# Map stage of a fused image block on one Trainium2 core: the second norm's broadcast and scaling move into the convolution, the fc2 products between the transposes

## Chip, core and metric

The kernel runs on one core of one Trainium2 chip. The metric is the time of one execution on the device in microseconds (us). The kernel before was timed three times; its time is the median of these runs.

## What is computed

The input is an image batch `x` (2, 96, 256, 256). A layer norm over channels is followed by windowed attention on overlapping 16x16 patches; then comes the part that this change touches, a per-pixel network with a depthwise convolution, and at last a small quantized network. Cut to the part that matters:

```python
y  = _layernorm(tok2, norm2_w, norm2_b)              # the "second norm", over 96 channels
y  = _gelu(y @ fc1_w + fc1_b)                        # fc1: 96 -> 192
dw = _gelu(depthwise_conv_5x5(y) + dw_b)             # 192 channels
tok2 = (y + dw) @ fc2_w + fc2_b + tok2               # fc2: 192 -> 96
x  = x + tok2                                        # outer residual
t  = x_tokens;  n = (t - mean(t)) / sqrt(var(t) + eps)   # the "third norm"
h  = relu(q_acc(q_mul(n) @ q_mul(W1).T) + q_mul(b1))     # 96 -> 384, fp8 products
x  = t + q_acc(q_acc(q_mul(h) @ q_mul(W2).T) + q_mul(b2))
```

## The kernel before

Three stages follow one another: `norm_stage`, `attention_stage` and `map_stage`. Only `map_stage` is touched. It works through the two images in 52 strips of 10 rows (26 for each image). The program of every engine is written out by hand: the order of the calls is the order of the work, and the engines meet through semaphores (`wait_ge`, `then_inc`). The loop runs over u = 0 to 50, the 52nd strip stands behind it.

One turn of the loop has a `first_half` and a `second_half`. It finishes strip u and, at places named `beside(...)`, prepares strip v = u + 1.

`first_half` on TensorE (`pe`):
- 12 products of fc1 for the pixels themselves (L1299), ScalarE puts them through Gelu into `Z` (L1391). Beside them run the variance sums of the second norm of strip v (`var2`, L1139).
- 6 groups (`NCG`) of 64 convolution matmuls as the profile counts them (L1312), in PSUM banks 0 and 1 or 2 and 3, with ScalarE's Gelu into `Z2` behind each (L1397). `gather2` (L1145) lies behind the first group. VectorE meanwhile turns the standard deviations into three bf16 parts of the reciprocal (`parts`, L1486 to L1493, the last one signals `dve_parts2`).
- 7 groups of transposes (L1328: six of 8, one of 4), alternating between banks 4, 5 and banks 6, 7. Behind each, VectorE adds the transposed convolution to `Z` (`back`, L1553, two instructions a group). A transpose group waits for the `back` of the group two before it.

`second_half` on TensorE:
- 6 products `fc2` (L1165, banks 0 and 1, `add_fc2` on VectorE at L1513 behind each) and between them 7 `spread2` (L1154, four bf16 matmuls each, banks 5 and 6), the broadcast of the reciprocals of the second norm of strip v. Behind each `spread2` VectorE scales two rows into `XN` (`scale2`, L1506). A `spread2` waits for the `scale2` two before it.
- The third norm: `mean3` (L1173), `centre3` on VectorE (L1518), squares on ScalarE (L1366), `var3` (L1179), `gather3` (L1185), the parts of the reciprocal on VectorE, `spread3` (L1191).
- The quantized network (`hidden` L1199, `output` L1207), and beside all of the third norm and this network the 26 `windows` (L1220) of strip v: fc1 on patches for the convolution, which ScalarE puts through Gelu into `Y1` (L1382).

SyncE stores the finished strip (L1048), once a strip. GpSimd adds the residuals (L1092, L1099) and copies the fc2 constant row (`means`, L1103). Before the loop the strip 0 is normed alone, with `spread2` and `scale2` following one another without other work.

The order of the calls in the second half before:

```python
fc2(nx, 0, n1)
fc2(nx, 1, n1)
beside(spread2, 0, 1)
fc2(nx, 2, n1)
beside(spread2, 2)
...
fc2(nx, 5, n1)
beside(spread2, 5, 6)
mean3(half3, n5, nx, 0)
mean3(half3, n5, nx, 1)
beside(windows, 0, 1)
```

Of the kernel before, what the change touches and what calls it, by code (L numbers as in the profile page):

```python
# [881 lines left out]
NF = TO // FT  # L882
XF = 43
NX = (W + XF - 1) // XF
NL = RI * W // FT
# [8 lines left out]
def map_stage(nc, x, n2w, n2b, fc1w, fc1b, dww, dwb, fc2w, fc2b, w1, b1, w2, b2, ident, pick, rep, spread, taps, inside,  # L894
# [3 lines left out]
    with ctx:  # L898
# [218 lines left out]
        def _(pe):  # L1117
# [106 lines left out]
            def second_half(n1, n5, nx, half3, v):  # L1224

                def beside(piece, *js):
                    if v is not None:
                        for j in js:
                            piece(v, j)

                fc2(nx, 0, n1)
                fc2(nx, 1, n1)
                beside(spread2, 0, 1)
                fc2(nx, 2, n1)
                beside(spread2, 2)
                fc2(nx, 3, n1)
                beside(spread2, 3)
                fc2(nx, 4, n1)
                beside(spread2, 4)
                fc2(nx, 5, n1)  # L1240
                beside(spread2, 5, 6)
                mean3(half3, n5, nx, 0)
                mean3(half3, n5, nx, 1)
                beside(windows, 0, 1)
                mean3(half3, n5, nx, 2)
                var3(n5, 0)
                beside(windows, 2)
                mean3(half3, n5, nx, 3)
                var3(n5, 1)
                beside(windows, 3)  # L1250
                mean3(half3, n5, nx, 4)
                var3(n5, 2)
                beside(windows, 4)
                var3(n5, 3)
                var3(n5, 4)
                beside(windows, 5)
                gather3(n1)
                beside(windows, 6)
                pe.wait_ge(dve_parts3, n1)
                spread3(n5, 0)  # L1260
                beside(windows, 7, 8)
                spread3(n5, 1)
                hidden(n5, 0)
                beside(windows, 9, 10, 11)
                spread3(n5, 2)
# [20 lines left out]
            def first_half(n13, n12, n6, n14, v):  # L1286

                def beside(piece, *js):
                    if v is not None:
# [14 lines left out]
                for q in range(NCG):  # L1304
# [32 lines left out]
            windows(0, *range(2 * NG))  # L1337
            with pe.Fori(0, nstrip - 1) as u:
                v = pe.snap(u + 1)
                first_half(pe.snap(u * (2 * NG)), pe.snap(u * (2 * NZ)), pe.snap(u * NCG), pe.snap(u * 14), v)  # L1340
                second_half(v, pe.snap(u * NF), pe.snap(u * NX), half_of(pe, u), v)
            last = nstrip - 1
            first_half(last * 2 * NG, last * 2 * NZ, last * NCG, last * 14, None)
            second_half(last + 1, last * NF, last * NX, half_of(pe, last), None)

        @block.scalar
        def _(act):
# [54 lines left out]
            def second_half(n1, n5, v):  # L1402
                def beside(*rs):
                    if v is not None:
                        windows(v, *rs)

                square3(n5, 0)
                square3(n5, 1)
                for j in range(2, NF):
                    beside(j - 2)  # L1410
                    square3(n5, j)
                beside(3)
                act.wait_ge(pe_rep3, n1)
                A.activation(STD3[:, :], P[0:C, 4, CV:2 * CV], ACT.Sqrt, bias=EPS[:, 0:1]).then_inc(act_std3, 1)

                beside(4, 5, 6, 7, 8)
                hidden16(n5, 0)
                beside(9, 10, 11)
                hidden16(n5, 1)
# [30 lines left out]
        def _(dve):  # L1450
# [104 lines left out]
            def first_half(n7, steps2, v):  # L1555
                if v is None:
                    back(n7, *range(NB))
                    return
                sum2(v)
                dve.wait_ge(act_std, v + 1)  # L1560
                parts(STD, RB[0], CV, steps2, dve_parts2)
                back(n7, *range(NB))

            def second_half(n1, n5, nx, half3, steps3, v):
                def beside(piece, *js):
                    if v is not None:
                        for j in js:
                            piece(v, j)

                dve.wait_ge(pool_x, n1)  # L1570
                add_fc2(half3, nx, 0)
                add_fc2(half3, nx, 1)
                beside(scale2, 0, 1)
                add_fc2(half3, nx, 2)
                beside(scale2, 2)
                add_fc2(half3, nx, 3)
                beside(scale2, 3)
                add_fc2(half3, nx, 4)
                beside(scale2, 4)
                add_fc2(half3, nx, 5)  # L1580
                beside(scale2, 5, 6)
                for j in range(NF):
                    centre3(half3, n5, j)
                sum3(n1, n5)
# [15 lines left out]
            with dve.Fori(0, nstrip - 1) as u:  # L1600
                v = dve.snap(u + 1)
                steps2 = dve.snap(u * (2 * VSTEPS) + (1 + VSTEPS))
                first_half(dve.snap(u * NB), steps2, v)
                second_half(v, dve.snap(u * NF), dve.snap(u * NX), half_of(dve, u), dve.snap(steps2 + VSTEPS), v)
            last = nstrip - 1
            steps3 = last * 2 * VSTEPS + 1 + VSTEPS
            first_half(last * NB, None, None)
            second_half(last + 1, last * NF, last * NX, half_of(dve, last), steps3, None)

# [65 lines left out]
```

## Time and profile before

| What | Value |
|---|---|
| Median of 3 runs | 8434.09 us (8430.1 to 8454.12) |
| Profiled execution, its time | 8441.3 us |
| Its span, first to last instruction | 8439.5 us |
| Mean granted TensorE clock | 0.975 of full speed |
| TensorE busy | 7670.8 us, 91% of the span |
| VectorE, ScalarE, GpSimd busy | 4919.9, 4683.4, 2161.9 us |

The span is cut into 40 slices on the profile's page. The attention stage ends in slice 19; the map stage fills the rest. All times in the rows below are counted in us from the span's start, and the line numbers are those of the kernel before. PE is TensorE, PEld its weight loads, DVE VectorE, ACT ScalarE, POOL GpSimd, SP SyncE.

### The profile page before, as it was taken

What the parts mean: (1) busy time and instruction counts of PE and PEld (TensorE: products, weight loads), DVE (VectorE), ACT (ScalarE), POOL (GpSimd) and SP (SyncE); (2) the same over time, 40 slices, a digit from 0 to 9 for tenths busy, and PEclk for the clock granted to TensorE, in tenths of its full rate; (3) what the DMA queues carried; (4) which work ended last, traced back from release to release, by engine and by line L of the source; (5) the groups of instructions that cost most, each with busy time, mean ns of one, the idle gap of its engine ahead of it and who ended that gap; (6) DMA issues with size and microseconds to landing.
All of it is one profiled execution on the core that took longest, in us unless ns stands there. A gap on an engine that the chain in (4) does not pass through costs nothing.

```text
span 8439.5 us, 205332 instructions
## 1 busy us (share of the span) xinstructions
PE 7670.8 (91%) x77004; PEld 4600.6 (55%) x77004; DVE 4919.9 (58%) x8231; ACT 4683.4 (55%) x7546; POOL 2161.9 (26%) x1712
## 2 busy tenths in 40 slices
PE   8969999999999999996989898989989898989898
PEld 3335555555455555554666666666666666666665
DVE  7867777777777777775344444444444444444444
ACT  6636555566565565653555454545454545455554
POOL 0023434434343343342112121212121212111111
PEclk9979999999999999997999999999999999999999
DMA  7734444444344443432111111111111111111110
GB/s 213 231 99 103 95 100 98 98 98 99 92 106 96 99 102 92 105 93 72 33 43 37 43 37 43 37 43 37 43 37 40 39 36 44 33 43 35 43 37 26
DMA packets 403125, 611.55 MB, mean 72 GB/s; under 512 B 95641, under 2 KB 338171, under 8 KB 377695
## 3 DMA queue, kind: packets, MB, share of 16 engines
q1 hardware_dynamic: 402639, 604.98, 28.9%
q8 instruction: 316, 5.18, 0.3%
q14 instruction: 170, 1.39, 0.1%
HBM read 395.33 MB, written 166.64 MB: 67 GB/s over the span
## 4 chain that ended last, share of the span: by engine, by line
PE 30%; DVE 10%; ACT 8%; issue 5%; DVEq 0%; SPq 0%; DMA 0%; ACTq 0%; POOLq 0%; POOL 0%
PE P L1299 6%; PE P L1165 6%; PE P L1312 5%; ACT H L1372 4%; PE P L1220 4%; DVE H L1538 3%; PE P L1173 3%; DVE H L1531 2%; PE P L1328 2%; DVE Z L1553 2%; PE P L1139 2%; ACT Z L1397 1%; ACT L1397 1%; ACT L1360 1%; PE P L1199 1%
## 5 line engine op out<-in xcount | busy, mean ns | idle before, releaser
L820 DVE TENSOR_REDUCE NM<-P 128x4 f32<-128x1024 f32 x1444 | 1764.8, 1222 | 596.3 <-PE P L654 591.7
L768 ACT ACTIVATE PROB<-P 128x1024 f32<-128x1024 f32 x1444 | 1400.2, 1021 | 1025.0 <-PE P L669 1025.0
L1220 PE MATMUL P<-FC,XN 97*126 97x192 f32 x5408 | 1099.0, 342 | 15.7 <-ACT Y L1382 14.8
L1220 PEld LDWEIGHTS P<-FC,XN 97*126 97x126 f32 x5408 | 941.3, 196 | 168.2 <-issue 77.8
L669 PE MATMUL P<-QF,KS 32*128 32x256 f32 x11552 | 834.5, 403 | 111.0 <-DVE QF L815 110.4
L1366 ACT ACTIVATE SQ<-Z 96x512 f32<-96x512 f32 x260 | 163.8, 630 | 1286.3 <-DVE Z L1518 1286.3
L669 PEld LDWEIGHTS P<-QF,KS 32*128 32x128 f32 x11552 | 525.4, 185 | 635.7 <-DVE QF L815 572.7
L505 POOL TENSOR_TENSOR Y<-XHS,RNS 96x512 f32<-96x512 f32 x304 | 600.6, 2003 | 811.8 <-DMA RNS<-rnorm 513.9
L677 PE MATMUL P<-PROB,V 128*32 128x256 f32 x11552 | 776.9, 386 | 1.4 <-ACT PROB L768 1.4
L1382 ACT ACTIVATE Y<-P 126x384 f32<-126x384 f32 x1352 | 704.1, 569 | 109.3 <-PE P L1220 104.2
L1099 POOL TENSOR_TENSOR T<-T,Y 96x512 f16 (+1 forms) x260 | 299.5, 1152 | 1720.0 <-DVE Y L1542 1720.0
L1103 POOL COPY Z<-T 1x2560 f32 (+1 forms) x52 | 236.9, 4555 | 1892.6 <-PE P L1165 1892.6
L1312 PE MATMUL P<-Y,WC 127*64 127x52 f32 x19968 | 625.2, 223 | 28.3 <-ACT Z L1397 28.3
L1312 PEld LDWEIGHTS P<-Y,WC 127*64 127x64 f32 x19968 | 598.9, 138 | 63.1 <-ACT Z L1397 34.9
L1553 DVE TENSOR_TENSOR Z<-P,Z 96x400 f32<-96x400 f32 (+1 forms) x728 | 342.6, 533 | 432.5 <-PE P L1328 432.5
L654 PE MATMUL P<-KB,QB 32*128 32x256 bf16 x5776 | 563.9, 272 | 20.1 <-DVE KB L810 16.9
L1299 PE MATMUL P<-XN,FC 97*96 97x440 f32 x1248 | 540.2, 554 | 0.7 <-ACT Y L1382 0.7
L645 PEld LDWEIGHTS P<-WQKV,Y 97*128 97x128 f32 x2888 | 377.5, 190 | 298.2 <-issue 298.2
L1165 PE MATMUL P<-Z,FC 97*96 97x430 f32 (+1 forms) x1248 | 499.4, 529 | 41.8 <-DVE Z L1553 41.8
L645 PE MATMUL P<-WQKV,Y 97*128 97x128 f32 x2888 | 515.4, 301 | 0.0
L1372 ACT ACTIVATE H<-P 128x1536 f16<-128x1536 f32 x260 | 377.4, 1451 | 238.7 <-DVE H L1538 182.8
L552 POOL TENSOR_TENSOR EDGE<-OS,RBC 128x160 f32<-128x160 f32 (+2 forms) x152 | 74.9, 493 | 1677.1 <-DMA RBC<-sums 1661.0
(152 smaller groups left out, 11706.8 us busy)
## 6 DMA issues: line engine op xcount, KB each, us to landing
RBC<-sums SPq DMA_DIRECT2D x456, 160.0 KB, 3.1
X<-x2map SPq DMA_DIRECT2D x52, 1344.0 KB, 8.3
XHS<-xhat SPq DMA_DIRECT2D x76, 768.0 KB, 6.2
RNS<-rnorm SPq DMA_DIRECT2D x38, 1536.0 KB, 9.4
x2map<-XHS SPq DMA_DIRECT2D x76, 768.0 KB
T<-in_x SPq DMA_DIRECT2D x52, 960.0 KB
out<-T SPq DMA_DIRECT2D x52, 960.0 KB, 4.9
X<-in_x SPq DMA_DIRECT2D x32, 1536.0 KB, 8.9
```

What stands on the lines that cost most here:

```text
L505: G.tensor_tensor(Y[0:C, x, :], XH[0:C, s % 2, :, x].rearrange("c r w -> c w r"), RN[:, :, x].rearrange("c r w -> c w r"), ALU.mult).then_ ...
L645: v = T.matmul(P[:, B_OV, PT + half * 128:PT + half * 128 + 128], yf[:, win(j, half * 128, half * 128 + 128)], WQKV[:, 128:256], start=Tru ...
L669: m = T.matmul(P[:, B_ST[h], half * PT:(half + 1) * PT], KS[hr, win(j, half * 128, half * 128 + 128)], QF[hr, :], start=True, stop=True)
L677: m = T.matmul(P[32 * h:32 * h + 32, B_OV, 0:PT], V[:, par, half, 32 * h:32 * h + 32], PROB[:, par, h, half * PT:(half + 1) * PT], start=( ...
L768: A.activation(PROB[:, par, u:u + 2, :], P[:, B_ST[u]:B_ST[u] + 2, :], ACT.Exp, scale=DQ ** -0.5).then_inc(act_exp, 1)
L820: V_.tensor_reduce(NM[:, :, :].rearrange("p a (u d) -> p u a d", d=32)[:, 2 * i:2 * i + 2, :, DQ], P[:, B_S[0]:B_S[0] + 2, :].rearrange("p ...
L1165: m = M.matmul(P[0:C, j % 2, 0:px.stop - px.start], FC2[0:C + 1 - half, half, :], Z[0:C + 1 - half, half, px], start=(half == 0), stop=(ha ...
L1220: m = M.matmul(P[0:KW, 5 + (r + 2) % 3, i * MLP:(i + 1) * MLP], xnf[:, RI * WX * w:RI * WX * w + KW], FC1[:, :], start=True, stop=True)
L1299: M.matmul(P[0:C, 6 + k % 2, 0:(x1 - x0) * RO], FC1[:, half * C:(half + 1) * C], XN[:, 2 + x0:2 + x1, 2:2 + RO], start=True, stop=True).th ...
L1312: m = M.matmul(P[64 * half:64 * half + 64, 2 * (q % 2) + i // GP, (i % GP) * NWIN:(i % GP + 1) * NWIN], WC[:, (half * C + c) * MW:(half * ...
L1372: A.activation(H16[:, :, :], P[:, 0:3, :], ACT.Copy).then_inc(act_h, 1)
L1382: A.activation(Y1[0:KW, :, 2 * r:2 * r + 2], P[0:KW, 5 + (r + 2) % 3, 0:2 * MLP].rearrange("p (w c) -> p c w", w=2), ACT.Gelu).then_inc(ac ...
```

## The change

On TensorE the 7 `spread2` leave the stretch of `fc2` and stand behind the last three groups of the convolution (0 and 1, then 2 and 3, then 4, 5 and 6). The transposes now wait for all 7 `scale2` of strip v, since they reuse banks 5 and 6. From the third group of transposes on, one `fc2` follows each group: it waits for the `back` of the group before. The two `windows` 0 and 1 stand ahead of the first `mean3`, and each later one up to 6 moves one place forward, so that `windows` 6 is issued ahead of `gather3`. VectorE does the 7 `scale2` ahead of `back`, and each `add_fc2` behind a `back`. ScalarE takes `windows` 0 ahead of the first square.

```diff
@@ second_half, TensorE
-                fc2(nx, 0, n1)
-                fc2(nx, 1, n1)
-                beside(spread2, 0, 1)
...
-                fc2(nx, 5, n1)
-                beside(spread2, 5, 6)
+                beside(windows, 0, 1)
                 mean3(half3, n5, nx, 0)
                 mean3(half3, n5, nx, 1)
-                beside(windows, 0, 1)
+                beside(windows, 2)
                 mean3(half3, n5, nx, 2)
...
-                beside(windows, 5)
+                beside(windows, 6)
                 gather3(n1)
-                beside(windows, 6)
                 pe.wait_ge(dve_parts3, n1)
@@ first_half, TensorE
+                    if q >= NCG - 3:
+                        beside(spread2, *((0, 1), (2, 3), (4, 5, 6))[q - NCG + 3])
+
+                if v is not None:
+                    pe.wait_ge(dve_xn, v * NL + NL)
                 pe.wait_ge(act_conv, n6 + NCG)
-                if v is not None:
-                    hold(pe, pe_passed, act_std, v + 1)
                 for q in range(NB):
...
                     m.then_inc(pe_zt, 1)
+                    if q >= 2:
+                        pe.wait_ge(dve_z, n14 + 2 * q)
+                        fc2(nx, q - 2, n1)
                 pe.wait_ge(dve_z, n14 + 14)
+                fc2(nx, NX - 1, n1)
@@ second_half, ScalarE
+                beside(0)
                 square3(n5, 0)
                 square3(n5, 1)
                 for j in range(2, NF):
-                    beside(j - 2)
+                    beside(j - 1)
                     square3(n5, j)
-                beside(3)
+                beside(4)
@@ first_half, VectorE
+                if v is not None:
+                    sum2(v)
+                    dve.wait_ge(act_std, v + 1)
+                    parts(STD, RB[0], CV, steps2, dve_parts2)
+                    for j in range(NL):
+                        scale2(v, j)
                 dve.wait_ge(pool_x, n1)
+                for q in range(NB):
+                    back(n7, q)
+                    if q >= 3:
+                        add_fc2(half3, nx, q - 3)
+                for j in range(NB - 3, NX):
+                    add_fc2(half3, nx, j)
```

No matmul, vector or activation instruction is added or taken away; only their places change.

TensorE at the end of the convolution, in the loop (L1301 is the convolution in the changed file, L1154 is `spread2`, L1319 are the transposes, which were L1328):

```order
+L1154 MATMUL P<-RB,BSEL 96x128 x8
+L1295 REGISTER_ALU
+L1301 MATMUL P<-Y,WC 64x52 x32
+L1154 MATMUL P<-RB,BSEL 96x128 x8
+L1295 REGISTER_ALU
+L1301 MATMUL P<-Y,WC 64x52 x32
+L1154 MATMUL P<-RB,BSEL 96x128 x12
+L1313 REGISTER_ALU
+L1319 MATMUL P<-IDN,Z 96x128 x16
```

The last three groups of the convolution now each have a block of `spread2` behind them, the last block with three of them right ahead of the transposes.

TensorE from the third transpose group on (L1165 is `fc2`):

```order
-L1165 MATMUL P<-Z,FC 96x430 x4
-L1154 MATMUL P<-RB,BSEL 96x128 x8
+L1319 MATMUL P<-IDN,Z 96x128 x8
+L1322 REGISTER_ALU
 L1165 MATMUL P<-Z,FC 96x430 x2
-L1154 MATMUL P<-RB,BSEL 96x128 x4
+L1319 MATMUL P<-IDN,Z 96x128 x8
+L1322 REGISTER_ALU
 L1165 MATMUL P<-Z,FC 96x430 x2
```

Where a `spread2` stood between two `fc2`, a transpose group and a wait now stand.

TensorE at the first `mean3` (L1173; L1220 are the `windows`):

```order
 L1165 MATMUL P<-Z,FC 96x410 x2
-L1154 MATMUL P<-RB,BSEL 96x128 x8
+L1214 ISA
+L1220 MATMUL P<-FC,XN 126x192 x4
 L1173 ISA
 L1173 MATMUL P<-T,MEANW 96x512
 L1173 ISA
 L1173 MATMUL P<-T,MEANW 96x512
-L1214 ISA
-L1220 MATMUL P<-FC,XN 126x192 x4
+L1220 MATMUL P<-FC,XN 126x192 x2
```

Two window pairs now stand between the last `fc2` and the first mean, in place of the last two `spread2`.

## Rows read from the trace of the kernel before

**Rows 1.** The page: span, and busy time of the engines.
```profile
span 8439.5 us, 205332 instructions
...
PE 7670.8 (91%) x77004; PEld 4600.6 (55%) x77004; DVE 4919.9 (58%) x8231; ACT 4683.4 (55%) x7546; POOL 2161.9 (26%) x1712
```

**Rows 2.** Timeline, SyncE's queue: stores of strips (start us, us, engine, line).
```profile
4193.53 0.36 SPq L1048 DMA_DIRECT2D out<-T  x1
...
5978.87 0.35 SPq L1048 DMA_DIRECT2D out<-T  x1
6064.06 0.36 SPq L1048 DMA_DIRECT2D out<-T  x1
6147.56 0.35 SPq L1048 DMA_DIRECT2D out<-T  x1
...
8273.59 0.36 SPq L1048 DMA_DIRECT2D out<-T  x1
```

**Rows 3.** Busy time by stretch: from:to, length, PE, PEld, DVE, ACT, POOL, PEclk.
```profile
6035.00:6037.70 2.70, 1.74 (x15) 1.70 (x16) 1.51 (x5) 1.53 (x4) 0.00 (x0) 1.00 0.00 0
6037.80:6041.20 3.40, 3.40 (x13) 2.75 (x12) 1.07 (x3) 2.42 (x3) 0.00 (x0) 0.50 0.00 0
...
6120.00:6124.00 4.00, 2.86 (x22) 2.55 (x23) 2.34 (x7) 2.46 (x6) 0.00 (x0) 1.00 0.00 0
```

**Rows 4.** Timeline, TensorE, end of the convolution and transposes (idle before, releaser).
```profile
6080.26 5.81 PE L1312 MATMUL P<-Y,WC 127*64 127x52 f32 x192 [0.56 <-ACT Z L1397]
6087.12 1.92 PE L1328 MATMUL P<-IDN,Z 128*96 128x128 f32 x16 [1.05 <-ACT Z L1397]
6089.40 2.01 PE L1328 MATMUL P<-IDN,Z 128*96 128x128 f32 x16 [0.36 <-DVE Z L1553]
```

**Rows 5.** The chain in order of time, fc2 and spread2 (start us, us, what).
```profile
6098.52 0.45 PE P L1154 x8
6098.97 1.48 PE P L1165 x4
6100.45 0.22 PE P L1154 x4
```

**Rows 6.** Timeline, TensorE, from the last two spread2 to spread3.
```profile
6105.31 0.61 PE L1154 MATMUL P<-RB,BSEL 96*96 96x128 bf16 x8
6106.54 1.95 PE L1173 MATMUL P<-T,MEANW 96*96 x4 [0.63 <-DVE T L1513]
6108.33 1.47 PE L1220 MATMUL P<-FC,XN 97*126 97x192 f32 x8
6109.63 1.02 PE L1173 MATMUL P<-T,MEANW 96*96 x2
6110.59 0.43 PE L1179 MATMUL P<-SQ,SSEL 96*32 96x128 f32 x8
...
6117.44 0.38 PE L1185 MATMUL P<-VS,REP 128*96 128x128 f32 x2
...
6121.14 0.42 PE L1191 MATMUL P<-RB,BSEL 96*96 96x128 bf16 x4 [2.67 <-DVE RB L1493]
```

**Rows 7.** Timeline, VectorE: last part of the second norm, first two `back` groups.
```profile
6080.49 0.22 DVE L1493 CAST RB<-RCP 32x128 bf16<-32x128 f32 x1
6088.21 2.01 DVE L1553 TENSOR_TENSOR Z<-P,Z 96x400 f32<-96x400 f32 x4 [7.50 <-PE P L1328]
```

**Rows 8.** Groups of instructions, VectorE, one strip (busy us, mean ns, idle before).
```profile
L1506 DVE TENSOR_TENSOR XN<-X,P 96x512 f32<-96x512 f32 x7 | 4.6, 683 | 0.0
L1513 DVE SCALAR_TENSOR_TENSOR T<-P,NW,T 96x430 f32 (+1 forms) x6 | 3.9, 658 | 4.0 <-PE P L1165 3.9
```

**Rows 9.** Timeline before the loop: last spread2, scale2 and first windows of strip 0.
```profile
3995.91 0.66 PE L1154 MATMUL P<-RB,BSEL 96*96 96x128 bf16 x4 [0.18 <-DVE XN L1506]
3996.61 0.69 DVE L1506 TENSOR_TENSOR XN<-X,P 96x512 f32<-96x512 f32 x1 [0.15 <-PE P L1154]
...
3997.45 0.97 PE L1220 MATMUL P<-FC,XN 97*126 97x192 f32 x2 [0.88 <-DVE XN L1506]
```

More of the change, by code:

```diff
@@ L1229, in beside @@
                             piece(v, j)
-                fc2(nx, 0, n1)
-                fc2(nx, 1, n1)
-                beside(spread2, 0, 1)
[L1234 to L1239, printed above, removed]
-                fc2(nx, 5, n1)
-                beside(spread2, 5, 6)
+                beside(windows, 0, 1)
                 mean3(half3, n5, nx, 0)
                 mean3(half3, n5, nx, 1)
-                beside(windows, 0, 1)
+                beside(windows, 2)
                 mean3(half3, n5, nx, 2)
                 var3(n5, 0)
-                beside(windows, 2)
+                beside(windows, 3)
                 mean3(half3, n5, nx, 3)
                 var3(n5, 1)
-                beside(windows, 3)
+                beside(windows, 4)
                 mean3(half3, n5, nx, 4)
                 var3(n5, 2)
-                beside(windows, 4)
+                beside(windows, 5)
                 var3(n5, 3)
                 var3(n5, 4)
-                beside(windows, 5)
+                beside(windows, 6)
                 gather3(n1)
-                beside(windows, 6)
                 pe.wait_ge(dve_parts3, n1)
@@ L1284, in second_half, with first_half @@
                 output(n5, 4)
-            def first_half(n13, n12, n6, n14, v):
+            def first_half(n13, n12, n6, n14, nx, n1, v):
                 def beside(piece, *js):
@@ L1339, in _ @@
                 v = pe.snap(u + 1)
-                first_half(pe.snap(u * (2 * NG)), pe.snap(u * (2 * NZ)), pe.snap(u * NCG), pe.snap(u * 14), v)
-                second_half(v, pe.snap(u * NF), pe.snap(u * NX), half_of(pe, u), v)
+                nx = pe.snap(u * NX)
+                first_half(pe.snap(u * (2 * NG)), pe.snap(u * (2 * NZ)), pe.snap(u * NCG), pe.snap(u * 14), nx, v, v)
+                second_half(v, pe.snap(u * NF), nx, half_of(pe, u), v)
             last = nstrip - 1
-            first_half(last * 2 * NG, last * 2 * NZ, last * NCG, last * 14, None)
+            first_half(last * 2 * NG, last * 2 * NZ, last * NCG, last * 14, last * NX, last + 1, None)
             second_half(last + 1, last * NF, last * NX, half_of(pe, last), None)
@@ L1409, in second_half @@
                 for j in range(2, NF):
-                    beside(j - 2)
+                    beside(j - 1)
                     square3(n5, j)
-                beside(3)
+                beside(4)
                 act.wait_ge(pe_rep3, n1)
                 A.activation(STD3[:, :], P[0:C, 4, CV:2 * CV], ACT.Sqrt, bias=EPS[:, 0:1]).then_inc(act_std3, 1)
-                beside(4, 5, 6, 7, 8)
+                beside(5, 6, 7, 8)
                 hidden16(n5, 0)
@@ L1553, in back, with first_half, second_half @@
                         V.tensor_tensor(z, p[:, 0:nw, half, 0:MW], z, ALU.add).then_inc(dve_z, 1)
[L1555 to L1568, printed above, removed]
-                dve.wait_ge(pool_x, n1)
[L1571 to L1581, printed above, removed]
+            def first_half(n7, steps2, half3, nx, n1, v):
+                if v is not None:
[4 more added lines that the diff above has]
+                        scale2(v, j)
+                dve.wait_ge(pool_x, n1)
+                for q in range(NB):
[4 more added lines that the diff above has]
+                    add_fc2(half3, nx, j)
+            def second_half(n1, n5, half3, steps3):
                 for j in range(NF):
@@ L1602, in _ @@
                 steps2 = dve.snap(u * (2 * VSTEPS) + (1 + VSTEPS))
-                first_half(dve.snap(u * NB), steps2, v)
-                second_half(v, dve.snap(u * NF), dve.snap(u * NX), half_of(dve, u), dve.snap(steps2 + VSTEPS), v)
+                half3 = half_of(dve, u)
+                first_half(dve.snap(u * NB), steps2, half3, dve.snap(u * NX), v, v)
+                second_half(v, dve.snap(u * NF), half3, dve.snap(steps2 + VSTEPS))
             last = nstrip - 1
             steps3 = last * 2 * VSTEPS + 1 + VSTEPS
-            first_half(last * NB, None, None)
-            second_half(last + 1, last * NF, last * NX, half_of(dve, last), steps3, None)
+            half3 = half_of(dve, last)
+            first_half(last * NB, None, half3, last * NX, last + 1, None)
+            second_half(last + 1, last * NF, half3, steps3)
 def constants():
```

## Prediction, made before the changed kernel was run

> **What bounds the kernel now.** I read the page first: TensorE is busy 91% of the span and no other engine over 58% [rows 1]. The store of each strip then gives the beat of the map stage: from 4193.53 to 8273.59 lie 48 strips, 85.00 us each on average [rows 2]. They are not equal: 85.19 us from 5978.87 to 6064.06, 83.50 us to the next [rows 2]. The view by stretches shows why. From 6037.8 to 6041.2 the granted clock is 0.50, which is the 1.2 GHz level, for 3.4 us in which TensorE works without a pause [rows 3]; in the shorter strip the same place, 6120 to 6124, stays at 1.00, the 2.4 GHz level [rows 3]. So one fall to 1.2 GHz costs 85.19 - 83.50 = 1.69 us, and the average strip holds (85.00 - 83.50) / 1.69 = 0.89 of one. The fall comes just behind the longest idle time that TensorE has in a strip, the 2.67 us in which it waits for the parts of the third norm [rows 6]. Everywhere in this part of the strip TensorE is busy or waits for VectorE, so its own timeline is the path: it is the sum that I make, from the fourth group of the convolution to the third mean.
>
> **The change, part by part.** I count from the start of the fourth convolution group, 6080.26 [rows 4]. Before, the transposes start at 6.86 (6087.12) [rows 4] and the third `mean3` at 29.37 (6109.63) [rows 6]. Now the new order.
>
> *Spreads in the convolution.* Three groups take 5.81 us less the 0.22 us tail of the last matmul, 1.87 us each [rows 4]. Two `spread2` take 0.45 us [rows 5]. A change between matmuls of 64 or 32 columns and of 96 seems to cost: a mean takes (6108.33 - 6106.54) / 2 = 0.90 us, but 0.96 us where the 32-column `var3` comes next [rows 6]; I take 0.09 for each change. The parts are ready at 0.45 (6080.71) [rows 7], far ahead of the first `spread2` at 1.96, and each `scale2` of 0.68 us [rows 8] finishes beside the next group. So the last group ends at 5.60 + 2 x 0.63 = 6.86. What follows has no cover: `spread2` 4 starts at 6.95, its four matmuls end 0.39 later, `scale2` 4 starts 0.04 behind them (3995.91 + 0.66 to 3996.61 [rows 9]) and ends at 8.06; `spread2` 6 waits for it, runs 0.42 as `spread3` does after a wait [rows 6], and `scale2` 6 ends at 9.25. A matmul starts 0.15 behind a `scale2` (3997.30 to 3997.45 [rows 9]). The transposes start at 9.40: 2.54 later than before.
>
> *fc2 between the transposes.* The first two groups and their `back` are unchanged, and the second `back` ends 6090.22 - 6087.12 = 3.10 behind the first transpose [rows 4, 7]. The third group fits in ahead of that, so the first `fc2` starts at 9.40 + 3.10 + 0.15 = 12.65. From there TensorE has work all the time: five `fc2` of about 1.45 (1.48 with the change to `spread2`) and one narrower of 1.39 (410 columns in place of 430), 8.6 us in all [rows 5], and four more transpose groups, 28 at 0.11 (16 start in 1.65 us [rows 4]), 3.1 us. VectorE needs 1.0 us for a `back` and 0.66 us for an `add_fc2` [rows 7, 8] against 2.3 us of TensorE a group; only the fifth `fc2` waits some 0.2 us for its bank. The last `fc2` is issued by 24.6.
>
> *Windows ahead of the mean.* Before, the first mean started 6106.54 - 6105.31 = 1.23 us behind the issue of the last `fc2`, 0.63 us of it a wait for `add_fc2` [rows 6]. Two windows take 1.30 us [rows 6] and fill just this: the first mean starts at 26.0. Two means take 1.79 us and one window 0.65 us: the third mean starts at 28.46, against 29.37. **That is 0.91 us less a strip.** One window more is then behind us, but it is the one that used to lie in the wait for the parts: from `gather3` to `spread3` pass 6121.14 - 6117.44 = 3.70 us before and after, as this is a chain over ScalarE and VectorE. TensorE's idle time in it grows from 2.67 to about 3.3 us, which costs nothing in itself. ScalarE's windows move by one with it and it has no more to do before the root. GpSimd's copy and SyncE's loads are released earlier, never later. Without any clock term the change is worth 51 x 0.91 = 46 us.
>
> *The clock.* The fall behind the third norm stays, its cause being longer. It now comes in every strip (0.89 before), while its start can also lie inside the idle time, which hides part of it: 0.8 to 1.69 us, about 1.5 on average, as before (0.89 x 1.69 = 1.50). New is idle time ahead of the transposes: TensorE stands still about 0.6 us before `spread2` 6 and 0.9 us before the transposes, with 0.4 us of work between. The kernel before has 1.05 us there and then 0.36 [rows 4] with no fall, and 2.67 us elsewhere with one. The new place lies between these rows, so its price runs from 0 to a fall in each strip. A fall there catches the two transpose groups that everything waits for: 16 transposes would take 3.3 to 3.5 us in place of 1.75, part of it is absorbed where group three waits for `back`, and 1.1 to 1.4 us are left, 1.2 in the mean. I take the fall: two idle times so close leave TensorE idle for most of 2 us, right behind a stretch of small matmuls, and before, too, nearly each strip had its fall from one single idle time. The Trainium skill, "TensorE: Matmul & The Clock Gate", section "A second HAM failure mode: psum-queue depth-cycling", says that short idle times between groups of matmuls, if frequent, are enough to make the clock swing between its levels. By that rule the sum is that with the second fall, without it the one under B; no row here shows a fall behind short idle times, so the trace neither agrees nor disagrees.
>
> **Sum.** A strip: 83.50 - 0.91 + 1.50 + 1.2 = 85.3 us, against 85.00. Over 51 strips +15 us; the last strip, which has no `spread2` to move and keeps the interleaving, gives back about 1. The profiled execution took 8441.3 us, 7 above the median of 8434.09, well inside the spread of the runs; I put the difference on the median: **8448 us, +0.17%**. A measurement of this kernel can tell about 0.3% (25 us) from no change, so this is "the same", 8409 to 8459.
>
> **Rivals.**
> - *A, the forecast:* the gain of 0.91 is there and a second fall in nearly each strip eats it. 8448 us, itself 8425 to 8462, since the fall's cost depends on where it starts. Chance 0.45.
> - *B, no second fall:* 1.5 us idle in two pieces are too little to drop the clock. For it: 1.05 + 0.36 us did not. Then 83.50 - 0.91 + 1.45 = 84.04 a strip, 8434 - 49 = 8385 us. If the fall comes in half the strips, about 8415. Chance together 0.33.
> - *C, slower:* each change between transposes and `fc2` costs what the change to 32 columns costs. There are 11 in a strip. At 0.09 us that is 1.0 us a strip, and with the second fall 8448 + 51 = 8499 us; it decides from 0.02 us a change (8459). Against it: between `spread2` and `fc2`, both 96 columns like the transposes, the chain shows no gap [rows 5]. New waits also stand at each change, for semaphores that came 0.1 to 1 us before. Chance 0.22. The Trainium skill, same page, section "Architectural detail: the array is 16× 32×32, not 1× 128×128", says that TensorE pulls weight loads ahead of running matmuls. By that rule the price of C is 0; the trace agrees for `fc2` and `spread2` (four matmuls in 0.22 us).
>
> That the change does not do what it says is no case here: the order of the calls is the order of the work, and the rows of the order show it.
>
> **How the numbers follow.** Faster 0.33 (B), same 0.45 (A), slower 0.22 (C). The range leaves out the upper part of C and the lower edge of B: 8378 to 8480. The likeliest case alone is 8425 to 8462.
>
> **What would show it.** In the profile after: the transposes start 9.4 us behind the fourth convolution group with idle times of about 0.6 and 0.9 us ahead of them; the third mean at 28.5 in a strip whose clock stays at 1.00 there; the idle time ahead of `spread3` is 3.3 us; a second stretch at 0.50 lies on the transposes in nearly each strip, and the 16 first transposes last about 3.4 us there. Strips come every 85.3 us. If no strip shows 0.50 on the transposes and the beat is 84.0, B is right; if clean strips show the third mean later than 29.0, C is, and the gaps between L1319 and L1165 will hold it. I am wrong altogether if VectorE, not TensorE, turns out late in the interleaved part, or if the fall behind the third norm disappears.

## The result, and the profile after

| | before | after |
|---|---|---|
| Median of 20 runs each | 8436.94 us (8430.1 to 8454.12) | 8451.48 us (8441.07 to 8465.49) |
| Ratio of the times, 95% interval | | 1.0016 [1.0009, 1.0022] |
| Profiled execution, its span | 8439.5 us | 8446.9 us |
| Mean granted TensorE clock | 0.975 | 0.964 |

One run of the changed kernel, 19892.7 us, was disturbed; it is left out of the range and the ratio, and the median without it is 8450.84 us. The change makes the kernel 14.5 us slower (13.9 without that run). This is clear of the noise, but less than the 0.3% (25 us) called "the same". The page of the changed kernel answers to [rows 1]: TensorE is busy 61 us longer with the same number of matmuls.

```profile
span 8446.9 us, 205540 instructions
...
PE 7731.9 (92%) x77004; PEld 4678.1 (55%) x77004; DVE 4925.3 (58%) x8231; ACT 4691.9 (56%) x7546; POOL 2161.1 (26%) x1712
```

SyncE's queue in the timeline, the stores of strips (start us, us, engine, line), against [rows 2]:

```profile
4186.54 0.36 SPq L1048 DMA_DIRECT2D out<-T  x1
...
5978.61 0.35 SPq L1048 DMA_DIRECT2D out<-T  x1
6063.94 0.36 SPq L1048 DMA_DIRECT2D out<-T  x1
...
7429.28 0.36 SPq L1048 DMA_DIRECT2D out<-T  x1
```

The strips now take the same time to within 0.1 us, but for the first. From 4186.54 to 7429.28 lie 38 of them, 85.33 us each; there is no shorter one any more, where before one in ten took 83.50. From the first transposes of the map stage to those of the strip before the last, 50 strips, pass 4252.0 us before (4044.6 to 8296.7) and 4268.4 us after (4040.1 to 8308.5): 16.4 us more. From there to the end it is 142.8 and 138.4, which is 4.4 less. Against that the transposes lie 2.8 us later in each strip by the new order, the first one too. 16.4 + 2.8 - 4.4 = 14.8 us, close to the difference of the medians. (In this pair of executions the stages ahead, which the change does not touch, ran 7.4 us shorter.)

TensorE's timeline of the changed kernel, end of the convolution and transposes (start us, us, ..., idle before and releaser), against [rows 4]:

```profile
6080.14 2.08 PE L1301 MATMUL P<-Y,WC 127*64 127x52 f32 x64 [0.56 <-ACT Z L1393]
6082.15 0.65 PE L1154 MATMUL P<-RB,BSEL 96*96 96x128 bf16 x8
6082.73 2.08 PE L1301 MATMUL P<-Y,WC 127*64 127x52 f32 x64
6084.73 0.65 PE L1154 MATMUL P<-RB,BSEL 96*96 96x128 bf16 x8
...
6088.52 0.42 PE L1154 MATMUL P<-RB,BSEL 96*96 96x128 bf16 x4 [0.56 <-DVE XN L1503]
6089.81 1.95 PE L1319 MATMUL P<-IDN,Z 128*96 128x128 f32 x16 [0.86 <-DVE XN L1503]
6092.12 1.05 PE L1319 MATMUL P<-IDN,Z 128*96 128x128 f32 x8 [0.36 <-DVE Z L1550]
6093.00 1.67 PE L1165 MATMUL P<-Z,FC 97*96 97x430 f32 x4
```

The transposes start 9.67 us behind the fourth convolution group (forecast 9.40), with 0.56 and 0.86 us of idle time ahead of them (forecast 0.6 and 0.9). The 16 first ones take 1.95 us, about as long as at 2.4 GHz in [rows 4] (1.92). From `fc2` on the rows have no idle time. The same view further on in the strip before, whose transposes start at 6004.47, against [rows 6]:

```profile
6023.24 1.02 PE L1173 MATMUL P<-T,MEANW 96*96 x2
...
6031.04 0.38 PE L1185 MATMUL P<-VS,REP 128*96 128x128 f32 x2
6034.75 0.66 PE L1191 MATMUL P<-RB,BSEL 96*96 96x128 bf16 x4 [3.33 <-DVE RB L1490]
```

The third mean starts 9.67 + 6023.24 - 6004.47 = 28.44 us behind the fourth convolution group; the forecast was 28.46. The idle time ahead of `spread3` is 3.33 (forecast 3.3). But `spread3` takes 0.66 us there, 0.42 in [rows 6]. The view by stretches says why (from:to, length, PE, PEld, DVE, ACT, POOL, clock, ...), against [rows 3]:

```profile
6002.00:6006.00 4.00, 2.58 (x28) 2.28 (x27) 2.32 (x4) 0.86 (x1) 0.00 (x0) 1.00 0.00 0
6031.50:6033.60 2.10, 0.00 (x0) 0.00 (x0) 1.49 (x4) 2.06 (x4) 0.00 (x0) 1.00 0.00 0
6033.70:6040.40 6.70, 5.65 (x22) 4.89 (x23) 2.28 (x6) 2.34 (x5) 0.00 (x0) 0.50 0.00 0
...
6119.10:6125.70 6.60, 5.62 (x22) 4.86 (x23) 2.21 (x6) 2.25 (x5) 0.00 (x0) 0.50 0.00 0
```

On the transposes (6002 to 6006) the clock is at its upper level, so the second fall of the forecast does not exist. The known fall behind the third norm has changed instead. It begins inside the idle time, 1.1 us ahead of `spread3`, and TensorE stays at 1.2 GHz for 6.8 us, where it was 3.4 us before. In the next strip it starts 85.33 us later, at the same place.

### The profile page after: what moved, and what is told of

It is laid out like the page before. It is cut to its first block, busy times and chain, and to the rows that moved or that the text cites. A ratio compares the mean times of both kernels' runs of the same rounds, so it can differ in the third digit from the quotient of the medians.

```text
span 8446.9 us, 205540 instructions
## 1 busy us (share of the span) xinstructions
PE 7731.9 (92%) x77004; PEld 4678.1 (55%) x77004; DVE 4925.3 (58%) x8231; ACT 4691.9 (56%) x7546; POOL 2161.1 (26%) x1712
## 4 chain that ended last, share of the span: by engine, by line
PE 33%; DVE 8%; ACT 7%; issue 4%; DVEq 0%; DMA 0%; SPq 0%; ACTq 0%; POOLq 0%; POOL 0%
PE P L1288 6%; PE P L1220 5%; PE P L1165 5%; PE P L1301 5%; ACT H L1368 4%; PE P L1319 3%; DVE H L1535 3%; PE P L1173 3%; DVE H L1528 2%; PE P L1139 2%; PE P L1154 1%; DVE XN L1503 1%; PE P L1191 1%; PE P L1199 1%; ACT L1393 1%
## 5 line engine op out<-in xcount | busy, mean ns | idle before, releaser
L1220 PE MATMUL P<-FC,XN 97*126 97x192 f32 x5408 | 1145.2, 352 | 15.8 <-ACT Y L1378 14.9
L1220 PEld LDWEIGHTS P<-FC,XN 97*126 97x126 f32 x5408 | 992.8, 205 | 188.0 <-issue 98.8
L1301 PE MATMUL P<-Y,WC 127*64 127x52 f32 x19968 | 646.5, 223 | 28.3 <-ACT Z L1393 28.3
L1301 PEld LDWEIGHTS P<-Y,WC 127*64 127x64 f32 x19968 | 607.1, 138 | 71.1 <-ACT Z L1393 34.9
L1165 PE MATMUL P<-Z,FC 97*96 97x430 f32 (+1 forms) x1248 | 497.2, 527 | 0.1
L1528 DVE TENSOR_SCALAR H<-H,BF 128x512 f16<-128x512 f16 x780 | 228.5, 349 | 406.2 <-ACT H L1368 406.2
```

The costliest lines, as they stand in the source:

```text
L1165: m = M.matmul(P[0:C, j % 2, 0:px.stop - px.start], FC2[0:C + 1 - half, half, :], Z[0:C + 1 - half, half, px], start=(half == 0), stop=(ha ...
L1220: m = M.matmul(P[0:KW, 5 + (r + 2) % 3, i * MLP:(i + 1) * MLP], xnf[:, RI * WX * w:RI * WX * w + KW], FC1[:, :], start=True, stop=True)
L1301: m = M.matmul(P[64 * half:64 * half + 64, 2 * (q % 2) + i // GP, (i % GP) * NWIN:(i % GP + 1) * NWIN], WC[:, (half * C + c) * MW:(half * ...
```

## The experiments

A stretch at 1.2 GHz is called a fall, and a strip or a kernel without one is called clean. Where a fall starts and how long it lasts comes from the granted clock in the view by stretches. All counts are of the 51 strips of the loop. The last strip, which runs behind the loop with nothing beside it, is left out; every kernel here has falls of 13 us and more in it. The runs are shown in three groups, each with the kernel before timed beside it (8437.05, 8439.9 and 8438.65 us).

### First group: what makes the fall longer?

Two theories on the doubled fall stood against each other. L: the idle time has grown from 2.67 to 3.33 us, and its length sets the fall's. T: the new idle times ahead of the transposes have a part in it.

**`windows` 6 back behind `gather3`**, which restores the idle time of 2.67 us (`windows` 2 to 5 move one place back too):

```diff
-                beside(windows, 2)
                 mean3(half3, n5, nx, 2)
                 var3(n5, 0)
-                beside(windows, 3)
+                beside(windows, 2)
...
-                beside(windows, 6)
+                beside(windows, 5)
                 gather3(n1)
+                beside(windows, 6)
```

> The changed kernel, but windows 6 stand behind gather3 again (windows 2 to 5 one place later), so that TensorE's idle time ahead of spread3 is 2.67 us in place of 3.33 us. The work of a strip is the same: a strip without a fall of the clock is expected at about 82.5 us. Theory L (the fall behind the third norm became twice as long, 6.8 us, because the idle time ahead of it grew): the fall is 3.4 us again and costs 1.5 to 1.7 us, strips of 84.1 us on average, 8385 us in all. Theory T (the idle time ahead of the transposes is enough for a fall of its own as soon as the first one is shorter): stretches at 0.50 on the transposes in most strips, strips near 85.3 us, 8445 us, no gain.

Measured: 8444.82 us, ratio 1.0007 [0.9997, 1.0018]. The timeline of SyncE (stores) has strips of two lengths in one execution:

```profile
4357.42 0.36 SPq L1048 DMA_DIRECT2D out<-T  x1
4439.57 0.35 SPq L1048 DMA_DIRECT2D out<-T  x1
4524.45 0.36 SPq L1048 DMA_DIRECT2D out<-T  x1
...
5974.19 0.35 SPq L1048 DMA_DIRECT2D out<-T  x1
6059.52 0.36 SPq L1048 DMA_DIRECT2D out<-T  x1
```

82.15 us is a clean strip, 84.88 the next, and later ones are all 85.33. Four stretches of this kernel:

```profile
4217.20:4220.50 3.30, 3.30 (x18) 3.08 (x16) 2.10 (x4) 0.00 (x0) 0.00 (x0) 0.50 0.85 213
4247.90:4251.30 3.40, 3.40 (x14) 2.73 (x13) 1.24 (x2) 1.14 (x2) 0.00 (x0) 0.50 0.00 0
4301.00:4304.50 3.50, 2.99 (x25) 2.71 (x26) 2.03 (x5) 0.00 (x0) 0.00 (x0) 1.00 0.58 131
6029.70:6036.40 6.70, 6.49 (x25) 5.71 (x26) 1.52 (x3) 2.56 (x4) 0.00 (x0) 0.50 0.00 0
```

And two places in TensorE's timeline:

```profile
4216.27 4.49 PE L1319 MATMUL P<-IDN,Z 128*96 128x128 f32 x24 [0.86 <-DVE XN L1503]
...
6029.91 0.66 PE L1191 MATMUL P<-RB,BSEL 96*96 96x128 bf16 x4 [2.67 <-DVE RB L1490]
```

The time is the one that T gave (8445), but its falls are not there. L is wrong: with 2.67 us of idle time the fall lasts 6.8 us too (6029.7 to 6036.4), once it starts ahead of `spread3`. T is right only in that there can be a fall on the transposes (4217.2 to 4220.5). A strip with it has a 3.4 us fall behind the third norm as well: 84.88 = 82.14 clean + 1.69 + 1.05, so a fall on the transposes costs 1.05 us, if the short one costs here what it costs before. Three of this kernel's strips have one, and in the changed kernel only the very first strip. The seven strips from the first long fall on last 84.87, 85.10, 85.22, 85.27, 85.30, 85.30 and 85.33 us, and the fall starts 28.65, 29.12, 29.35, 29.47, 29.53, 29.56 and 29.59 us behind the first transpose. As long as a strip is shorter than 85.33, the next fall comes that much later in its strip, less of it is hidden in the idle time, and the next strip is longer. At 85.33 this stands still.

**`windows` 7 moved from behind `spread3` 0 to behind `gather3`:**

```diff
                 gather3(n1)
+                beside(windows, 7)
                 pe.wait_ge(dve_parts3, n1)
                 spread3(n5, 0)
-                beside(windows, 7, 8)
+                beside(windows, 8)
```

> The changed kernel, with windows 7 issued between gather3 and spread3, so that the idle time is 2.67 us and 0.65 us of work more is out of the way: a strip without a fall at about 81.9 us. Theory L: falls of 3.4 us, 1.6 us each, strips of 83.5 us, 8355 us in all. Theory T: falls on the transposes in addition, in some half of the strips or more (1.2 us each) and strips of 84.5 us or so, 8405 us. If neither the idle time nor its length matters and the fall stays at 6.8 us: 84.7 us, 8415 us.

Measured: 8436.29 us, 1.0001 [0.9991, 1.0011], more than any of its three forecasts. With 2.67 us of idle time 43 falls behind the third norm last 6.8 us and 8 last 3.4. Their starts part them: all long ones start at most 0.35 us behind the start of `spread3`, all short ones at least 0.35 us behind it. The strips mostly take 85.25 us, but this kernel does not come to rest: the fall starts some 0.08 us later in each strip, until a short one comes (strips of 83.6 and 84.0 us) or one on the transposes beside the long one (86.2 us, four strips; the first strip has one too). The mean strip is 85.04, 0.29 less than in the changed kernel, and the moved window alone saves 0.26 by clean strips (second group). So this small saving shows, while the change's 0.95 does not. One of the falls on the transposes, by stretches (the transposes start at 4557.18):

```profile
4557.20:4560.50 3.30, 3.30 (x16) 3.15 (x17) 1.05 (x2) 0.00 (x0) 0.00 (x0) 0.50 0.54 135
```

**All `fc2` behind all transposes,** everything else as in the changed kernel:

```diff
-                    if q >= 2:
-                        pe.wait_ge(dve_z, n14 + 2 * q)
-                        fc2(nx, q - 2, n1)
                 pe.wait_ge(dve_z, n14 + 14)
-                fc2(nx, NX - 1, n1)
+                for j in range(NX):
+                    fc2(nx, j, n1)
```

> Only one part of the change undone: the six fc2 stand behind all transposes again, the rest as in the changed kernel. TensorE then has the three waits of about 0.3 us between transposes and 0.8 us ahead of the first fc2 again: a strip without a fall at 82.5 + 1.7 = 84.2 us. Theory L: idle 3.33 us ahead of spread3, fall of 6.8 us, 2.9 us: 87 us a strip, 8530 us. Theory T: the idle times ahead of and between the transposes now add up and there is a fall on them in most strips; 86.5 to 87 us, 8520 us, too, but with two stretches at 0.50 a strip. If the fall costs only 1.5 us: 85.7 us, 8470 us.

Measured: 8527.21 us, 1.0108 [1.0091, 1.0124]. Stores, then TensorE's `fc2` in the timeline:

```profile
6015.63 0.35 SPq L1048 DMA_DIRECT2D out<-T  x1
6101.76 0.36 SPq L1048 DMA_DIRECT2D out<-T  x1
6189.38 0.35 SPq L1048 DMA_DIRECT2D out<-T  x1
```
```profile
6135.92 8.86 PE L1165 MATMUL P<-Z,FC 97*96 97x430 f32 x24 [0.81 <-DVE Z L1548]
```

The waits for `back` that the interleaving covers are open again (0.81 us ahead of the first `fc2`, and two of 0.27 ahead of transposes). Strips with a short fall take 86.13 us, so a clean one would take 86.13 - 1.69 = 84.44, 1.9 more than in the changed order. Those with a long fall (22 of 51) take 87.6 to 87.8. The time is the one that L gave (8530), but by luck: L had a long fall in every strip. Rival C, by which switching between transposes and `fc2` costs more than it brings, has fallen. Here too the long falls start ahead of `spread3` or at most 0.31 us behind its start, the short ones from 0.35 us on.

**The windows' move alone, on the kernel before** (`windows` 0 and 1 ahead of the first mean, the later ones one place forward, ScalarE's the same):

```diff
                 beside(spread2, 5, 6)
+                beside(windows, 0, 1)
                 mean3(half3, n5, nx, 0)
                 mean3(half3, n5, nx, 1)
-                beside(windows, 0, 1)
+                beside(windows, 2)
```

> The kernel before with one part of the change alone: windows 0 and 1 ahead of the first mean, and windows 6 ahead of gather3. They cover the wait of 0.63 us ahead of the mean: a strip without a fall at 83.50 - 0.63 = 82.9 us. The idle time ahead of spread3 grows to 3.33 us here too, and nothing is changed ahead of the transposes (1.05 us idle). Theory L: the fall becomes 6.8 us long in most strips and costs 2.4 to 2.9 us, strips of 85.3 to 85.7 us, 8450 us or more: the part alone is no gain. Theory T (the length of that idle time is of no matter): fall as before, 1.5 us, strips of 84.4 us, 8405 us.

Measured: 8624.9 us, 1.0222 [1.0205, 1.0239]: far from what was expected. TensorE's timeline, and a stretch right behind:

```profile
6013.29 2.00 PE L1220 MATMUL P<-FC,XN 97*126 97x192 f32 x8 [1.69 <-DVE XN L1507]
6015.09 3.15 PE L1173 MATMUL P<-T,MEANW 96*96 x4
```
```profile
6014.30:6017.60 3.30, 3.30 (x7) 1.60 (x6) 0.56 (x1) 0.49 (x1) 1.57 (x1) 0.50 0.89 209
```

In the old order `scale2` 6 is the last thing in the stretch of `fc2`, and all windows wait for it. Ahead of the mean TensorE stands idle 1.69 us for it, and the whole third norm comes later; a second fall follows (in 50 strips), and the strips take 88.6 us, or 89.2 where the fall behind the third norm is a long one (12 of 51; those start 2.0 us or more ahead of `spread3`). The windows can only go ahead of the mean because the change has `scale2` finished in the convolution. The parts of this change can't be priced one at a time on the kernel before.

### Second group: the idle times filled

If the clock is what takes the gain, the gain must appear where it doesn't fall. Two f32 matmuls of 512 columns are put into the wait for the third norm's parts. Their output is not read by anyone.

```diff
+            def fill(bank, *ns):
+                for n in ns:
+                    M.matmul(P[0:C, bank, 0:n], MEANW[:, :], WC[0:C, 0:n], start=True, stop=True)
...
                 gather3(n1)
+                fill(0, 512, 512)
                 pe.wait_ge(dve_parts3, n1)
```

> The changed kernel with two idle-filling matmuls of 96x96x512 f32 behind gather3, 0.9 us each, whose output nobody reads. They shorten TensorE's idle time ahead of spread3 from 3.33 to about 1.6 us and end ahead of the parts, so no work is late. Theory I (the idle time in the third norm is what drops the clock): the fall there disappears; what is left are the falls ahead of the transposes that the first strips of the run with windows 6 behind gather3 showed (each with 1.1 us of cost, in up to half of the strips): 82.2 to 82.8 us a strip, 8295 to 8325 us. Theory P (the chip drops the clock for something else than idle time, such as small matmuls or a fixed beat): the falls stay, 85.3 us a strip, 8450 us.

Measured: 8343.41 us, 0.9889 [0.9873, 0.9906]. Stores:

```profile
6006.36 0.36 SPq L1048 DMA_DIRECT2D out<-T  x1
6088.93 0.35 SPq L1048 DMA_DIRECT2D out<-T  x1
6173.16 0.36 SPq L1048 DMA_DIRECT2D out<-T  x1
```

82.55 us is the clean strip of the changed kernel, taken from strips whose fill ends ahead of `spread3`. A third of the strips still have a fall behind the third norm, with 1.60 us of idle time left: 14 a short one (84.23 us), and 3 a long one together with one on the transposes (86.97). The mean is 83.30, and the time missed the forecast (8295 to 8325) by these falls. Theory P of the expectation, by which the falls stay whatever the idle time, has fallen: 33 of 51 strips have none.

**The same with the idle times ahead of the transposes filled too:**

```diff
-                        beside(spread2, *((0, 1), (2, 3), (4, 5, 6))[q - NCG + 3])
+                        beside(spread2, *((0, 1), (2, 3), (4, 5))[q - NCG + 3])
...
                 if v is not None:
+                    fill(4, 256)
+                    spread2(v, NL - 1)
+                    fill(4, 384)
                     pe.wait_ge(dve_xn, v * NL + NL)
```

> As the run before, with two more idle-filling matmuls, of 256 columns ahead of spread2 6 and of 384 columns ahead of the transposes, 0.45 and 0.65 us, both shorter than the waits of 0.56 and 0.86 us. Theory I: no strip has a fall any more, every strip lasts 82.2 us, 8290 us in all, 1.7% less than the kernel before. Theory P: falls stay, 8450 us. If the filling matmuls themselves delay spread2 6 or the transposes, by up to 0.3 us a strip, 8305 us.

Measured: 8340.5 us, 0.988 [0.9864, 0.9897], mean strip 83.16; forecast was 8290 without any fall. No strip has a fall on the transposes any more, where the kernel without this second fill had four, nor a long one; but 19 in place of 14 have a short one, and the time is the same within the intervals. So the idle times ahead of the transposes, in which the forecast saw the trouble, have a fall of their own in a few strips and no measurable part in the total.

**The kernel before with the third norm's wait filled** (the fill as above, behind `windows` 6):

> The kernel before with the two filling matmuls between windows 6 and spread3 alone: idle 2.67 us becomes 0.9 us. Theory I: no fall left, every strip 83.50 us, as its five strips without a fall were: 8437 - 51 x 1.50 = 8360 us. Theory P: no change, 8437 us. Beside the kernel with both places filled it gives what the change is worth at a clock that stays up: 83.50 - 82.2 = 1.3 us a strip, or the 0.9 us of the sum.

Measured: 8359.76 us, 0.9904 [0.9887, 0.992]. Stores, and one strip by stretches:

```profile
6108.62 0.35 SPq L1048 DMA_DIRECT2D out<-T  x1
6192.11 0.36 SPq L1048 DMA_DIRECT2D out<-T  x1
```
```profile
6100.00:6183.00 83.00, 76.25 (x779) 50.97 (x778) 36.88 (x80) 45.04 (x72) 15.91 (x7) 1.00 0.16 41
```

Each strip takes 83.50 us, with no fall, as forecast (8360 us); `fill` leaves 0.96 us of idle time here. It is also the clean strip without the fill [rows 2], so the fill itself costs nothing. This gives the comparison that the two kernels themselves can't give: clean, the change is worth 83.50 - 82.55 = 0.95 us a strip, and 0.91 was forecast.

**`windows` 7 behind `gather3`, with both fills** (the edits of the second and sixth experiment together):

> The changed kernel, both places filled, and windows 7 behind gather3 ahead of the filling matmuls: 0.65 us of real work moves into the idle time, what is left idle is 0.9 us. Theory I: no fall, 82.2 - 0.65 = 81.5 us a strip if TensorE bounds the stretch behind spread3, 8255 us; 82.2 us, 8290 us, if the chain over ScalarE and VectorE bounds it there. Theory P: 8436 us as without the filling.

Measured: 8294.19 us, 0.9829 [0.9812, 0.9845]. From one store to the next pass 82.28 us (6069.07 to 6151.35), 82.29 on average: 0.26 less than without the move. No strip has a fall. This is the lesser of the two gains forecast (8290 us).

### Third group: the best version, and the parts priced without falls

**`windows` 6 and 7 both behind `gather3`, with fills** (the third norm's now `fill(0, 512, 256)`):

> Windows 6 and 7 behind gather3 (windows 2 to 5 one place later than in the changed kernel), then filling matmuls of 512 and 256 columns, and both fillings ahead of the transposes. The strips without a fall lasted 82.14 us with windows 6 behind gather3 and 82.55 us with windows 6 ahead of it; windows 7 behind it gained 0.26 us there. If both gains add, 81.9 us a strip without a fall, 8275 us; if they are the same gain, 82.15 us, 8290 us. A fall in a third of the strips would add 30 us.

Measured: 8273.66 us, 0.9812 [0.9796, 0.9828]. Stores; TensorE up to `spread3` (L1195 here); one strip by stretches:

```profile
6064.46 0.35 SPq L1048 DMA_DIRECT2D out<-T  x1
6146.33 0.36 SPq L1048 DMA_DIRECT2D out<-T  x1
```
```profile
6118.00 1.46 PE L1185 MATMUL P<-WC,MEANW 96*96 96x512 f32 x4
6120.19 0.42 PE L1195 MATMUL P<-RB,BSEL 96*96 96x128 bf16 x4 [0.73 <-DVE RB L1498]
```
```profile
6100.00:6182.00 82.00, 78.03 (x788) 52.12 (x787) 37.50 (x81) 45.55 (x72) 15.89 (x7) 1.00 0.16 41
```

This is what the sum of both gains had forecast (8275 us). The version beats both kernels, by 1.9% and 2.1% (8273.66 / 8451.48). A strip takes 81.88 us. The two windows in the wait are worth 82.55 - 81.88 = 0.67 us: 0.26 for `windows` 7, and 0.41 for `windows` 6 by the clean strip of the first experiment (82.55 - 82.14).

**The windows in their old order, with both fills** (`windows` 0 and 1 behind the second mean, 6 behind `gather3`, ScalarE as before):

> The changed kernel with both places filled, and the windows in the order of the kernel before: the part of the change on the windows undone alone. By the sum of the prediction the third mean then starts at 24.6 + 1.23 + 1.79 + 1.30 = 28.92 us in place of 28.46: a strip without a fall lasts 82.55 + 0.46 = 83.0 us, 8365 to 8375 us with falls in a third of the strips, 8340 without. If the windows part is worth nothing, 82.55 us as with it.

Measured: 8347.23 us, 0.989 [0.9873, 0.9906]. Strips of 83.20 us, clean (6106.39 to 6189.59), against 83.0 forecast. The windows' part of the change is worth 83.20 - 82.55 = 0.65 us. Of it, `windows` 0 and 1 ahead of the mean bring 83.20 - 82.14 = 1.06, and `windows` 6 ahead of `gather3` takes 0.41 of that away.

**All `fc2` behind the transposes, with both fills** (the edit of the third experiment on the kernel of the sixth):

> The changed kernel with the six fc2 behind all transposes, both places filled. The same order without filling gave 86.12 us for strips with a short fall, 84.43 us without it. With the fall gone: 84.4 us a strip, 8405 us in all, if interleaving is worth 1.9 us a strip; 84.2 us, 8395 us, if it is worth the 1.7 us that the waits and the mean of before add up to.

Measured: 8482.05 us, 1.0056 [1.0039, 1.0073]. The forecast of 8405 us had no falls in it. 1.60 us of idle time are left ahead of `spread3`, and 34 of 51 strips have a fall there: 26 a short one (86.13 us), 8 a long one (87.8). The 17 clean strips take 84.46 us on average (one of them from 6080.98 to 6165.45). The interleaving is worth 84.46 - 82.55 = 1.91 us, as by the third experiment (1.89). So the other parts together cost 1.91 - 0.95 = 0.96 us a strip (the transposes start 2.8 us later). The windows' place needs them, as the fourth experiment shows; whether the interleaving does was not tried.

## Why the prediction was right or wrong

**The number was right, but by luck in part: one of its two reasons was wrong.** 8448 was forecast and 8451.48 measured, inside the range and inside "the same".

- *Spreads in the convolution:* right. The transposes start at 9.67 instead of 9.40. Of the 0.27, 0.22 arise ahead of `spread2` 4, which starts at 7.17 in place of 6.95: a pair of `spread2` and the group behind it take 2.58 us (6082.15 to 6084.73), where the sum had 0.63 + 1.87 = 2.50. The chain of `scale2` behind came out as summed, to 0.05.
- *`fc2` between the transposes:* right. There are no idle times there, and the third mean lies at 28.44 (28.46 forecast). Of **C**, the switching cost, nothing was found. The rule cited there from the Trainium skill ("TensorE: Matmul & The Clock Gate", section "Architectural detail: the array is 16× 32×32, not 1× 128×128"), that weight loads are pulled ahead of running matmuls, fits these rows; no run here tests it by itself.
- *Windows ahead of the mean, sum 0.91:* right. The whole change was worth 0.95 in clean strips. That `windows` 6 ahead of `gather3` costs nothing was not: there it costs 0.41 us a strip, by the clean strips of the first experiment.
- *The fall behind the third norm, "about 1.5 on average, as before":* **this is the step that failed.** The fall there does not stay as it was. It starts ahead of `spread3` in all strips and lasts 6.8 us in place of 3.4; it costs 85.33 - 82.55 = 2.78 us, and not 1.5. That a start inside the idle time *hides part of the fall* was the argument for a lower price. The hiding is there: of 6.83 us, 1.12 pass in the idle time, and half of the other 5.71, which TensorE works through at half clock, is 2.85, near the 2.78. But such a fall lasts twice as long, and that outweighs it. That the longer idle time "costs nothing in itself" is not refuted: with 2.67 us of it, in the first experiment, the fall lasts as long as with 3.33. The kernel before shows it once, in the first strip of the map stage, whose fall starts 0.15 us ahead of `spread3` (first row below: the stretch; second: TensorE's timeline). The prediction had not used that strip.

```profile
4078.60:4085.20 6.60, 6.52 (x25) 5.76 (x26) 1.39 (x3) 2.67 (x5) 0.00 (x0) 0.50 0.00 0
```
```profile
4078.68 0.66 PE L1191 MATMUL P<-RB,BSEL 96*96 96x128 bf16 x4 [2.67 <-DVE RB L1493]
```

- *"I take the fall" (the second one, on the transposes, 1.2 us in nearly each strip):* wrong. The changed kernel has it in its first strip alone. Its size was good: where it occurs, in the first experiment, it costs 1.05 us. In the second experiment five strips have it and in the fifth (the first with a fill) four, but none in the five kernels in which the idle times of 0.56 and 0.86 us are filled too. The Trainium skill ("TensorE: Matmul & The Clock Gate", section "A second HAM failure mode: psum-queue depth-cycling") says that frequent short idle times can make the clock swing; these strips agree with that, but it gives no measure of how often.
- *Sum:* forecast 83.50 - 0.91 + 1.50 + 1.2 = 85.29; measured 83.50 - 0.95 + 2.78 = 85.33. The extra clock cost was 1.28 us a strip, and 1.2 had been put down, at another place. So the number is no proof of the reasoning; that both mechanisms cost about as much was luck.
- *The last strip:* gives back 1.8 us, where about 1 was forecast: from its first transposes to the end pass 62.0 us before and 60.1 after. That is near the 1.9 of the interleaving, which it keeps. Of the 4.4 us of the first section the rest is, in the main, the 2.8 by which the other strips' transposes start later; the last strip has no spreads ahead of them.
- **B** (no second fall, 84.04 a strip) was right that there is none, and wrong by the same unseen doubling. The "what would show it" part left this case out: no fall on the transposes, yet 85.3 a strip.

**Why 85.33.** In the changed kernel and in the one before, the falls of successive strips start 85.33 us apart. Before, the strips with a short fall take 85.17 to 85.19, so that it starts some 0.15 us later in each; after about ten strips it is missed once (the strip of 83.50 in [rows 2]). With the long fall a strip can reach 85.33, and there it stays. In the changed kernel and the first experiment this is why neither the saving of 0.95 nor the other place of `windows` 6 (0.41) shows in the beat: a shorter strip is drawn out again by a fall of which less is hidden. The second experiment does not come to rest, and its mean strip is shorter by what it saves. All this is read from the starts of the falls; no run set a start by itself.

**What stays open.** Why the starts keep to 85.33 us, and why a fall that starts up to 0.35 us behind `spread3` lasts twice as long, was not settled; the runs show it and don't give the cause. Nor is it clear why with 1.6 us of idle time left a third of the strips keep a fall (two thirds in the last experiment), and why the second fill does not remove it. Kernels with 0.95 and 0.73 us left had none. No idle time between these was tried.

## What to carry to other kernels

Where the clock falls once per turn of a loop, the turn's length feeds back on where the fall starts, and a small saving of work can vanish in it: price a change by turns without a fall, and if there are none, make some by filling the idle time with unread matmuls. When a move changes the idle time ahead of a fall or the length of the turn, where the fall starts and how long it lasts must be forecast anew, from the whole turn and not from the idle time alone. Try the parts of a reordering on top of the change, not only on the kernel before: one part may stand on another, as the windows here stand on the earlier `scale2` (+2.2% alone, 0.65 us a strip less in its place).

## What was not expected of the hardware

- Extra TensorE work made the kernel faster: two unread matmuls of 512 columns a strip, 1.88 us of TensorE time, take 1.0% off the kernel before and 1.3% off the changed one (8343.41 / 8451.48).
- In the loop, falls behind the third norm last 3.4 or 6.8 us, nothing between. In the kernel before, after, and the first three experiments, all 85 short ones start at least 0.35 us behind the start of `spread3` (45, 0, 3, 8 and 29 of them), and all 162 long ones ahead of it or at most 0.35 us behind (1, 51, 45, 43 and 22), whatever the idle time (2.67 or 3.33 us). The other runs that have falls there keep to it too, with 1.60 us of idle time as well.
- In the kernel before and the changed one the falls of successive strips start 85.33 us apart. The changed kernel and the first experiment come to just this beat and stay there; the kernel before, with strips of 85.17, does not, and drops a fall about every eleventh strip.
